# A two-layer decoder kernel: first scores inside the query projection, two output products as rounded halves, shorter steps in the context mix

## The reference, cut to what matters

```python
x = x + L0_attn(layernorm(x))              # causal, 8 heads of 128, one shared K and V
x = x + L0_xattn(ctx, layernorm(x), mask)  # 16 heads of 64, keys and values from [norm(ctx), norm(latents)]
x = x + L0_ffn(layernorm(x))               # 8 experts, one chosen per row; gelu(x @ W1[e] + b1[e]) @ Wo + bo, layernorm
x = x + L1_attn(layernorm(x))              # causal, 16 heads of 64, one shared K and V
x = x + L1_xattn(layernorm(x), ctx, ctx)   # no softmax: the context enters through ctx^T ctx; layernorm
x = x + L1_ffn(layernorm(x))               # 4 experts, top 2, a shared FFN with low-rank corrections
# L0_xattn ends with:
weight = softmax(q k^T); out = (weight @ v).reshape(b, l, 1024); return out @ Wout
```

## Time and profile before

| | us |
|---|---|
| median of three runs | 1776.1 |
| the three runs | 1771.97, 1776.1, 9249.27 |
| profiled execution | 1779.62 |
| its span | 1777.8 |
| PE matmul busy | 1671.7 (94%) |
| DVE busy | 1022.1 (57%) |
| ACT busy | 750.2 (42%) |
| POOL busy | 530.4 (30%) |

### The profile page before, as it was taken

One profiled execution on the slowest core, in us unless ns is written; L12 is line 12 of the kernel. 1 busy time (PEld: TensorE's weight loads), 2 busy tenths in 40 slices (PEclk: granted clock), 3 DMA queues, 4 the chain that ended last, 5 costly groups with the idle time before them and its releaser, 6 DMA issues. The chain is left out here.

```text
span 1777.8 us, 32493 instructions
## 1 busy us (share of the span) xinstructions
PE 1671.7 (94%) x11198; PEld 1323.0 (74%) x11198; DVE 1022.1 (57%) x2461; ACT 750.2 (42%) x2126; POOL 530.4 (30%) x579
## 2 busy tenths in 40 slices
PE   7899899999999999999999987999988799977998
PEld 6687677777777777777777766889877677655666
DVE  5466466655666666566666554142264388757574
ACT  2255344444444444444444430343203477642221
POOL 1022223333333333333333324243420133444000
PEclk9999999999999999999999998999998899987999
DMA  3100300000000000000002004765210000020000
...
DMA packets 48805, 67.41 MB, mean 38 GB/s; under 512 B 11826, under 2 KB 42770, under 8 KB 46034
## 3 DMA queue, kind: packets, MB, share of 16 engines
...
q0 software_dynamic: 1536, 3.67, 0.6%
...
## 5 line engine op out<-in xcount | busy, mean ns | idle before, releaser
L697 POOL TENSOR_TENSOR l0x_p<-l0x_p,l0x_inv 112x488 f32<-112x488 f32 x256 | 251.8, 1005 | 472.6 <-DVE l0x_inv L791 472.6
L900 ACT ACTIVATE l0x_p<-l0x_s,l0x_low 112x488 f32<-112x488 f32 x256 | 178.3, 697 | 275.1 <-DVE l0x_low L780 274.6
L780 DVE CUSTOM_DVE_ANT_0 l0x_s<-l0x_score_ps,l0x_bias 112x488 f32<-112x488 f32 x256 | 160.1, 662 | 113.9 <-PE l0x_score_ps L1040 104.4
L767 DVE TENSOR_TENSOR l0x_kT_lo<-l0x_proj_ps,l0x_kT_hi 128x488 fp32r<-128x488 f32 x128 | 85.3, 667 | 106.3 <-ACT l0x_kT_hi L890 106.3
L1061 PEld LDWEIGHTS l0x_oT_ps<-l0x_pT,l0x_v 122*64 122x64 f32 x2048 | 100.7, 138 | 43.9 <-issue 32.6
L1061 PE MATMUL l0x_oT_ps<-l0x_pT,l0x_v 122*64 122x112 f32 x2048 | 127.9, 267 | 4.9 <-DVE l0x_pT L786 4.1
L1048 PE MATMUL l0x_pT_ps<-ident,l0x_p 112*122 112x112 f32 x1024 | 120.2, 260 | 0.4 <-POOL l0x_p L697 0.3
L1048 PEld LDWEIGHTS l0x_pT_ps<-ident,l0x_p 112*122 112x122 f32 x1024 | 107.0, 138 | 18.2 <-issue 6.0
L996 PE MATMUL l0x_proj_ps<-l0x_kvT_hi,l0x_wkv_hi 128*128 128x488 f32 x256 | 111.0, 434 | 2.9 <-DVE l0x_kvT_lo L755 2.9
L1904 POOL TENSOR_TENSOR l1a_pn<-l1a_p,l1a_inv 112x896 f32<-112x896 f32 x32 | 53.9, 1684 | 190.6 <-DVE l1a_inv L1933 190.6
L1989 ACT ACTIVATE l1a_p<-l1a_p,l1a_shift 112x112 f32<-112x112 f32 x256 | 95.4, 374 | 32.4 <-DVE l1a_shift L1927 32.4
...
## 6 DMA issues: line engine op xcount, KB each, us to landing
l0f_w<-in_l0f_w SPq DMA_DIRECT2D x21, 1024.0 KB
...
l0x_wkv<-in_l0x_wkv SPq DMA_DIRECT2D x2, 1024.0 KB, 9.0
...
```

What stands on the lines that cost most here:

```text
L697: nc.gpsimd.tensor_tensor(p[:, i % 2, a, :], p[:, i % 2, a, :], inv[:, i % 2, a:a + 1].broadcast_to([S, KEYS]), ALU.mult).then_inc(pn_read ...
L780: nc.vector.tensor_tensor_reduce(s_sb[:, h % 2, :], score_ps[0:S, h % 2, 0:KEYS], bias[:], -SCALE, 3.4e38, ALU.add, ALU.min, low[:, h:h + ...
L900: nc.scalar.activation(p[:, h // 2 % 2, h % 2, :], s_sb[:, h % 2, :], ACT.Exp, scale=-1.0, bias=low[:, h:h + 1], accum_out=total[:, h:h + ...
```

## The change

1. **l0_attention.** `score(0)` and `score(1)` are issued within the last quarter's query projection (before heads 0 and 4), with `softmax(0)`, `exp(0)`, `invert_sums(0)` and `normalise(0)` beside it; `softmax(1)` follows DVE's last copy. The second block no longer begins with them. `p` and `pn` are allocated earlier.
2. **l0_cross_attention.** The output product is done as rounded halves. `wout` is split during the first batch (ACT rounds a chunk a step, DVE subtracts); ACT's copy of `oT` writes `oT_hi`, and DVE has a new `split_oT`, twice a batch. In each step the transposes stand directly behind the scores, and `copy_pT` and `invert_totals` stand ahead of the splits of queries, keys and values. `wout` is staged in memory of the later gram context, whose loads wait for the split; `x1T` shares memory with `kvT`.
3. **l0_experts.** The second product of the tiles is done as rounded halves: per tile ACT makes two copies of 512 columns (`hT_hi`), DVE two subtractions (`split_tile`). `wo` is split at the start by ACT and POOL. z is scaled in place, so that `residual` waits for the store of two tiles before.
4. **l1_attention.** Both halves of `score(0)` stand at the head of the last quarter, with mask, shift, exp and sums of batch 0 beside the projection; `wo` (1 MB) is loaded in this block instead of beside the tiles. At the end ACT normalises group 0 for the next block.
5. **l1_context_mix, l1_experts.** POOL's additions are issued without waiting for this group's `x1`, and `add_bias(g+1)` stands ahead of `invert_output(g)`. `find_best` of group 2 moves to l1_experts.

```diff
 # l0_attention, PE and DVE in the last quarter of the query projection
+                        if q == Q - 1 and i == 0:
+                            score(pe, 0)
+                        elif q == Q - 1 and i == 4:
+                            score(pe, 1)
...
+                        if q == Q - 1 and i == 1:
+                            dve.wait_ge(late_w, 32)
+                            softmax(dve, 0)
+                        elif q == Q - 1 and i == 5:
+                            invert_sums(dve, 0)
+                softmax(dve, 1)
 # l0_cross_attention, DVE and ACT
+            def split_oT(b, n):
+                dve.wait_ge(oT_hi_ready, b * 2 + n + 1)
+                group = slice(4 * n, 4 * n + 4)
+                nc.vector.tensor_tensor(oT_lo[:, group, :].rearrange("p h s -> p (h s)"), oT_ps[:, 0, 0:4 * S],
+                                        oT_hi[:, group, :].rearrange("p h s -> p (h s)").bitcast(F32), ALU.subtract
+                                        ).then_inc(oT_lo_ready, 1)
...
+                    if i == 1 and not first:
+                        split_oT(b - 1, 1)
+                    elif i == 5:
+                        split_oT(b, 0)
+                    if i >= 1:
+                        copy_pT(b, i - 1)
+                    elif not first:
+                        copy_pT(b - 1, HP - 1)
+                    invert_totals(b, i)
 # l0_experts, DVE and PE
+            def split_tile(i):
+                for n in range(2):
+                    part = slice(n * FC // 2, (n + 1) * FC // 2)
+                    dve.wait_ge(hT_hi_ready, 2 * i + n + 1)
+                    nc.vector.tensor_tensor(hT_lo[:, i % 2, part], hT[:, part], hT_hi[:, i % 2, part].bitcast(F32),
+                                            ALU.subtract).then_inc(hT_lo_ready, 1)
...
-                    done = nc.tensor.matmul(y_ps[:, i % 2, 0:D], hT[:, i % 2, f, :], wo[:, f, :],
-                                            start=(f == 0), stop=(f == FC - 1))
+                        pe.wait_ge(hT_lo_ready, 2 * i + f // 4 + 1)
+                    hi, lo = hT_hi[:, i % 2, f, :], hT_lo[:, i % 2, f, :]
+                    nc.tensor.matmul(y_ps[:, i % 2, 0:D], hi, wo_hi[:, f, :], start=(f == 0), stop=False)
+                    nc.tensor.matmul(y_ps[:, i % 2, 0:D], hi, wo_lo[:, f, :], start=False, stop=False)
+                    done = nc.tensor.matmul(y_ps[:, i % 2, 0:D], lo, wo_hi[:, f, :], start=False, stop=(f == FC - 1))
 # l1_context_mix, POOL
-                    pool.wait_ge(x1_ready, b + 1)
+                    since(pool, x1_ready, b + 1 - GB)
...
-                invert_output(g)
                 if g + 1 < G:
                     add_bias(g + 1)
+                invert_output(g)
                 if g >= 2:
                     subtract_first(g - 2)
-            subtract_first(G - 2)
```

447 lines of the change are left out of this document (252 added, 195 removed).

## The result

| | before | after |
|---|---|---|
| median of four runs | 1774.26 | 1723.65 |
| lowest | 1771.97 | 1721.06 |
| profiled execution | 1779.62 | 1724.28 |
| its span | 1777.8 | 1722.4 |

The kernel became faster: the ratio of the times is 0.9717, interval 0.9696 to 0.9738. The medians lie 50.6 us apart, the two profiled spans 55.4 us. One of the four runs before took 9249 us; the medians are not touched by it. A second set of runs of the same changed kernel gave 1724.59 us (1722.4 to 1728.32).

The account below looks back on a forecast made before the run. PE, 94% busy, was taken as the bound: only time leaving its stream or its idle stretches counts. Five parts (-7.3, -8.6, -12.0, -7.7, -10.4) sum to -46.0 from 1779.6, forecasting 1733.6 us, range 1719 to 1752.

Parts of the forecast that it names:

- The rival's 1721.8: Rounded products, cross attention and tiles: matmuls go by passes, 107 ns each, 11.8 us more gained, 1721.8 us; chance 0.09.
- The price of a rounded product: Cross attention and tiles: 120 ns per rounded 256-column matmul, three 360 in place of 442 ns, a product 0.65 us shorter.
- Part 1: l0_attention: moving the first scores into the projection gives -7.3 us, ends 5 and 9.
- Part 2: l0_cross_attention: 16 rounded products by 0.65 us, less stalls, give -8.6 us, ends -14 and +1.
- In the steady parts PE is gapless, and there only cheaper matmuls help: Whole kernel, steady stretches: PE has no idle time, so only cheaper matmuls gain there; no size of its own.
- Part 3: l0_experts: 21 rounded tile products by 0.65 us, less about 1.6 lost on waits, give -12.0 us, ends -17 and -8.
- Part 4: l1_attention: the same move of first scores into the projection gives -7.7 us, ends -5 and -10.
- Part 5: Context mix: early normalisation 2.1, `update` 3.8, `find_best` 3.0 and clock 1.5 give -10.4 us, ends -5 and -15.
- A late chain in the cross attention: Cross attention: `split_oT` ahead of `copy_pT` stalls batches 0.7 us, part 2 gives nothing, 1742 us; chance 0.19.
- The starts give half: Parts 1, 4 and 5: lower clock or `exp` halves their gain, 12.7 us lost, 1746 us; chance 0.14.
- Blocking of VectorE and GpSimd in the tiles: l0_experts tiles: `split_tile` doubles beside POOL, a third of tiles stall by 1 us, 1741 us; chance 0.02.
- A floor of 240 ns for rounded matmuls: Rounded 256-column matmuls cost as much as 512-column ones, 2.2 us more per product, 1840 us, slower than before; chance 0.04.

Follow-up runs that it names:

- the transposes experiment: The changed kernel with the previous step's transposes put ahead of the scores in four of eight steps of the cross attention; 1744.14 us, ratio 0.9805.

## Why the prediction came out as it did

**The time.** 1733.6 us was forecast, 1723.65 measured: inside the range of 1719 to 1752 and on its lower side, 10 us too slow. On the profile's own base the sum said -46.0, and the trace has -55.3 (1779.6 to 1724.3). The rival's 1721.8 lies closer than the forecast, but its reason is refuted: it wanted 107 ns a matmul, and the traces have 120.

**The price of a rounded product: right.** 120 ns were taken from half of a 512-column row; 0.12 us is measured in the cross attention, in the tiles (1204.82, 1204.94, 1205.06 and so on) and in l0_attention, the third place, in the experiments that round its product. The term was mis-sized by the part that half a row can't show: a group's first matmul starts its successor 0.18 to 0.20 us later, so a product is 2.96 and not 2.88, and shorter by 0.59, not 0.65. In the cross attention the batch gained 0.65 in before's order all the same: the other 0.07 are in the transposes ahead of the product, a term that the sum did not have, so that this agreement is luck. The Trainium skill (FP8 and Floating Point Precision, TensorE Precision Notes) says that true float32 takes four passes; an estimate from it, three passes for the three rounded matmuls, makes the product 2.65 us. The trace does not agree: no kernel here went below 2.96.

**Part 1, l0_attention: right** (-8.3 for -7.3). The transposes came at 77.25 and 83.44 for 77.8 and 84.2. The better end of the bound held: the new wait is short, and the clock did not fall.

**Part 2, the cross attention: the step that failed is "In the steady parts PE is gapless, and there only cheaper matmuls help".** -15.2 for -8.6. The sum had 16 x 0.65 less stalls; of the 1.08 us a batch, the product is 0.6 and the order 0.43 to 0.48, over 15 batches some 7 us, which is the miss. The prediction looked at the order only for waits (will p be late?) and gave the reordering of PE's own steps no term. It did not look at what two neighbouring kinds of matmul cost each other, though the rows of before had it: projections of keys in two groups of six took 2.86 us for twelve. The expected stall of 0.1 a batch did not come either; `split_oT` (620 ns, as its row said 625) is waited for once, at the end of the block, 1.4 us.

**Part 3, the tiles: right** (-11.6 for -12.0), though its parts were not. "The transfers keep pace" was wrong: up to tile 5 nothing is gained (97.5 us before and after), where five or six products were counted with little loss. A later tile gained 0.58 and not 0.65. What filled the sum up again are 2.1 us of a transfer wait that went with the moved loads, and 1.5 behind the tiles, which is less than that stretch scatters among kernels with the same code (71.9 to 77.1 us). The hit of the sum is in part luck; which of the moved loads (`wo` of the next block, `wout`'s memory) did it was not tried. `split_tile` beside POOL went from 692 to 1225 ns at worst, with no effect: its chain was hidden, as argued.

**Part 4, l1_attention: right, 1.2 us too much** (-6.5 for -7.7). "The waits vanish" was the step that was too large: a wait of 2.2 us for the first `pT` copied by DVE came in place of the 5.4, with 3.4 us at the lower clock. Batch 1's transposes came 6.5 us earlier in the block, not 7.7. In two other traces, of the transposes experiment and of the one that normalises group 0 later, those 3.4 us are missing and the block takes 212.6 us, 8.5 less than before, so the size is known to 2 us only.

**Part 5, the mix: right in kind, 4 us too small** (-14.7 for -10.4). `update` was priced at 3.8 for two groups and is 3.8 to 4.7; it was doubled in three of the four groups (12 of 16 instructions), so that 3.8 for two is right in part by luck; the early normalisation at 2.1 and is 2.2 to 3.1. That leaves some 7 to 9 us for the move of `find_best` and the clock, where 4.5 were counted (3.0 and 1.5). The lower clock fell from 34.5 to 10.2 us there. If PE is busy for 0.84 of the 24.3 us that vanished, as in the last 13.7 us of the earlier trace rows, up to 10 us came back by this alone (an estimate from those rows; the 3.8 to 4.7 and the 2.2 to 3.1 above hold a part of it), where 1.5 was counted. So the term that was mis-sized is most likely the clock's, which no run shows by itself. How much belongs to `find_best` was not separated either; the wait at the end of the mix is 3.9 us before, 2.6 with `find_best` moved and POOL's order as before, and 1.1 after, so the 3.0 counted for `find_best` were not its alone. One statement ahead of the prediction was too wide: POOL's additions drop the wait for this group's `x1`, but the count they wait for instead is that of the group before, so only group 0 goes without a wait.

**The rivals.** A late chain in the cross attention: no wait for `oT_lo` or p in a steady batch. The starts give half: parts 1 and 4 gave 14.8 of 15.0. Blocking of VectorE and GpSimd in the tiles: it happens, 1225 ns, and is hidden. A floor of 240 ns for rounded matmuls: 120 measured.
